# Idle products on PE, a sum among the squares, and two moves in the first stage of a two-stage kernel

## The chip, the cores and the metric

One Trainium2 chip, one of its cores. The metric is the time of one execution in microseconds on the device. The engines are PE (matrix products), DVE (vector), ACT (scalar activations), POOL (GpSimd) and SP, whose queue issues most transfers. Each has its own list of instructions, and they meet only at semaphores.

## What is computed

A block of a network on u, 16 sequences of 512 tokens with 256 channels:

```
q, k, v = u Wq + bq, u Wk + bk, u Wv + bv          # per channel, along the sequence
k = causal_conv(k, k_kernel) + k_D * k             # 512 taps per channel
y = causal_conv(k * v, ssm_kernel) + k * v * D
x = layernorm(u + (y * q) Wo + bo)
h = square(relu(x W_fc))                           # 1024 hidden
z = h W_proj                                       # back to 256
spikes: five steps of mem = 0.9 mem + z - reset, counting how often mem > 1
out = layernorm(x + count / 5)
```

## The kernel before, in words

Every float32 factor of a product is scaled by a power of two and split into a high and a low float16 part, and three products (high by high, high by low, low by high) stand for one. The scales come from maxima over weights and data.

**First stage, projections of the first 32 channels.** u comes in eight pieces. DVE takes their maxima, POOL joins them, and DVE works out the scales (`d_scale`, `read_factor`, the scaled biases `bias_b`; lines 962 to 984). ACT then makes the high part of one piece after another (semaphore `u_hi`; line 455, for pieces 5 and 7 lines 451 and 453), and DVE makes the low parts (`split_u`, line 986), POOL those of pieces 5 and 7 (line 607). PE projects the tokens in four quarters of 96 products of 96 columns each (`project`, line 684), each as soon as its two pieces are split, in turn into PSUM banks 0 to 3 and 4 to 7. DVE reads each quarter with three operations: keys (line 1000), queries (1013), values (1000), `read_projection`. After the last quarter it copies the next chunk's weights from `wnext` to `wcur` (line 1022, semaphore `wcur_ready`), for which PE and SP's next load of weights wait. `windows1` masks windows of taps (line 1040).

**Second stage, convolutions.** The 256 channels go in 32 groups of 8 (`NG`). For each group PE does a quarter of the projection of a later chunk (96 products), 96 products of the first convolution (`conv1`, line 698) and 96 of the second for the group before (`conv2`). SP loads the windows of taps of group g + 2 when half of conv1(g) is through. The first four groups are written out on PE; the others are a hardware loop over pairs (`pair_of_steps`), in which each projection stands in an If with one form and an Else with another, 96 products each, and each is followed by 96 products of conv1 and 96 of conv2. DVE ends a group with `times_q`; on the last two groups lie also the maxima of the second stage's weights `wf_st`, `wp_st` (`max_abs`, line 932).

**Between the stages.** PE transposes the joined maxima (line 883), turns the first sequence (`turn_y`, eight transposes, line 773), projects it (`project_out`, line 795, 16 recorded products), while DVE works out the scales (lines 1138 to 1149). DVE's first sums (line 1225) wait for the first half of `project_out(0)` and stand behind the scales. Their moments, POOL's root, DVE's shift, ACT's norm and PE's `turn_x` follow one another before the first sequence's products.

**Third stage, 16 sequences.** For each, PE makes eight hidden tiles (`up`, line 817, six products of 512 columns each), ACT the relu (514), DVE the square (1199), ACT its high part (518), POOL its low part (631), and PE multiplies by W_proj (`down_first`, 32 products, then `down_second`, 16; line 824). ACT's list puts the high part of tile f behind the relu of tile f + 3 (`HI_LAG`). DVE compares z with five thresholds (`spikes`, lines 1207 and 1210), for each of two halves. `second_sum` (line 1217) with its moments (1158, 1163) finishes the sequence before, and stands behind the squares and ahead of the comparisons. In the last sequence DVE makes the low parts of the odd tiles (`h_part`, line 1188). `up` for tile f waits for the relu of tile f - 2, the square of tile f in the last sequence for low part f - 4.

Of the kernel before, what the change touches and what calls it, by code (L numbers as in the profile page):

```python
# [5 lines left out]
ALU = mybir.AluOpType  # L6
# [7 lines left out]
P = 128  # L14
B, L, D, F = 16, 512, 256, 1024
NI = L // P
DT = D // P
FT = F // P
# [3 lines left out]
NC = D // CH  # L22
G = 8
GPC = CH // G
NG = D // G
# [49 lines left out]
def build(nc, uT, u, wcat, wk_n, wv_n, bias, bo, k1, k2, kd1, kd2, woT, wfT, wpT, out):  # L75
# [11 lines left out]
    with ExitStack() as ctx:  # L87
# [15 lines left out]
        w_scale = sb("w_scale", [P, 6], F32)  # L103
# [310 lines left out]
        def _(act):  # L414
# [101 lines left out]
            def hidden_hi(i, f):  # L516
                act.wait_ge(square_ready, i * FT + f + 1)
                nc.scalar.activation(h16[:, 0, f], h_square[:, f % 4], ACT.Copy).then_inc(h_hi, 1)  # L518
# [3 lines left out]
            def body(i, r, left, turn=None):  # L522
                first = isinstance(i, int) and i == 0
                if not first:
                    act.wait_ge(down_done, i * 2)
                for f in range(FT + HI_LAG):
                    if f < FT:
                        hidden_relu(i, f)
                    if f >= HI_LAG:
                        hidden_hi(i, f - HI_LAG)  # L530
                if left > 1:
                    y_turn(i + 2)
                if left:
                    if not first:
                        act.wait_ge(sum2_ready, i)
                    norm(0, i + 1, 1 - r)
                    x_turn(i + 1, 1 - r)
                if not first:
                    if turn is not None:

                        act.wait_ge(stored[1 - r], 16 * turn)
                    norm(1, i - 1, 1 - r)
# [129 lines left out]
        def _(pe):  # L672
# [17 lines left out]
            def convolve(half, out, data, taps, done):  # L690
# [11 lines left out]
                            k += 1  # L702
                last.then_inc(done, 1)

            pe.wait_ge(ld_wcur, 16)
            for quarter in range(GPC):
                pieces = (quarter + 1) * NU // GPC
# [69 lines left out]
            def turn_y(i, r):  # L777
                if isinstance(i, int) and i == 0:
                    pe.wait_ge(y_first_ready, 2)
                else:  # L780
                    pe.wait_ge(y_seq_ready, i)
                if not isinstance(i, int) or i >= 2:
                    pe.wait_ge(x_lo, i - 1)
                    pe.wait_ge(x_hi, i - 1)
                turn(y_seq[:, r], y_turned)
# [93 lines left out]
                down_second(1)  # L879

            pe.wait_ge(id_done, 3)
            pe.wait_ge(part_max2_done, 1)
            nc.tensor.transpose(ps[0:3, 4, 0:P], part_max[:, cF:cF + 3], ident[:, :]).then_inc(turned2, 1)
            turn_y(0, 0)
            pe.wait_ge(spread2, 1)
            nc.tensor.transpose(ps[:, 5, 0:3], spread_max[0:3, :], ident[0:3, 0:3]).then_inc(all_max2_done, 1)
# [18 lines left out]
        def _(dve):  # L905
            links = [0]

            def link(ins):

                links[0] += 1  # L910
                ins.then_inc(vlink, 1)
                dve.wait_ge(vlink, links[0])
# [18 lines left out]
            def max_abs(dst, src, axis=AX.XY):  # L931
                link(nc.vector.tensor_reduce(dst, src, axis, ALU.max, apply_absolute_value=True))  # L932
# [21 lines left out]
            for n in range(NU):  # L954
# [15 lines left out]
            link(nc.vector.tensor_tensor(uw, d_unscale[:, 0:1], w_unscale[:, cW:cW + 1], ALU.mult))  # L970
            nc.vector.tensor_tensor(read_factor[:, 0:1], uw, d_scale[:, 1:2], ALU.mult)

            link(nc.vector.tensor_scalar(scratch[:, 0:1], d_scale[:, 2:3], d_unscale[:, 1:2], w_unscale[:, cK1:cK1 + 1], ALU.mult, ALU.mult))
            link(nc.vector.tensor_tensor(read_factor[:, 2:3], scratch[:, 0:1], uw, ALU.mult))
            nc.vector.tensor_scalar(read_factor[:, 3:4], d_unscale[:, 2:3], w_unscale[:, cK2:cK2 + 1], uw, ALU.mult, ALU.mult)
            nc.vector.tensor_scalar(bias_b[:, :, 1], bias_b[:, :, 1], scratch[:, 0:1], None, ALU.mult)
            nc.vector.tensor_scalar(bias_b[:, :, 2], bias_b[:, :, 2], d_scale[:, 0:1], w_scale[:, cW:cW + 1],
                                    ALU.mult, ALU.mult)
            nc.vector.tensor_scalar(bias_b[:, :, 0], bias_b[:, :, 0], d_scale[:, 1:2], None, ALU.mult
                                    ).then_inc(scales2, 1)  # L980
            dve.wait_ge(scales2, 1)

            def split_u(n):
                dve.wait_ge(u_hi, n + 1)
                cols = slice(n * UP, (n + 1) * UP)
# [30 lines left out]

            def read_values(quarter, r, chunk, banks=PA):
                read_scaled(1, vbuf, quarter, r, chunk, banks).then_inc(proj_read, 1)
                if quarter == GPC - 1 and chunk + 1 < NC:

                    dve.wait_ge(ld_wnext, 16 * (chunk + 1))
                    nc.vector.tensor_copy(wcur, wnext).then_inc(wcur_ready, 2)

            def read_projection(quarter, r, n, chunk, banks=PA):
                read_keys_queries(quarter, r, n, chunk, banks)
                read_values(quarter, r, chunk, banks)
# [40 lines left out]
            for quarter in range(GPC):  # L1067
                for n in range(quarter * NU // GPC, (quarter + 1) * NU // GPC):
                    if n not in POOL_PIECES:
                        split_u(n)  # L1070
                if quarter == 0:
                    dve.wait_ge(u_lo, 2)
                if quarter == 1:
                    windows1(0, 0)
                if quarter:
                    read_projection(quarter - 1, 0, quarter - 1, 0, PAS[(quarter - 1) % 2])
            read_projection(GPC - 1, 0, GPC - 1, 0, PAS[(GPC - 1) % 2])
            windows1(1, 1)
            dve.wait_ge(u_lo, NU - len(POOL_PIECES))
# [15 lines left out]
            def times_q(s, g):  # L1095
                dve.wait_ge(c2_half, 2 * g + 2)
                q = qy[:, bass.ds(g * GC, GC)]
                nc.vector.scalar_tensor_tensor(q, PC2[:, s % 2], read_factor[:, 3:4], q, ALU.mult, ALU.mult
                                               ).then_inc(y_ready, 1)
# [20 lines left out]
                    step(s, pair * PAIR, True, pair * 2)  # L1120
            for s in range(PAIR):
                step(s, NG - PAIR, s < GPC, NC - 2)
            times_q(PAIR - 2, NG - 2)
            dve.wait_ge(ld_wf, 16)
            max_abs(part_max[:, cF:cF + 1], wf_st)
            dve.wait_ge(ld_wp, 16)
            max_abs(part_max[:, cP:cP + 1], wp_st)

# [115 lines left out]
            def body(i, r, first, last):  # L1244
                if not last:
                    first_sum(i + 1, 1 - r)
                for f in range(FT):
                    square(i, f)
                    if f == 2 and not last:
                        norm_shift(0, i + 1)  # L1250
                    if last and f in (4, 6):
                        h_part(i, f - 3)
                if last:
                    h_part(i, 5)
                    h_part(i, 7)
                if not first:
                    second_sum(i - 1, 1 - r, isinstance(i, int) and i == 1)
                spikes(i, 0, range(0, len(theta)))
                if not first:
                    norm_shift(1, i - 1)  # L1260
                if not last:
                    split_x(i + 1, 1 - r)
                spikes(i, 1, range(0, len(theta)))
# [42 lines left out]
```

## Time and profile before

| | us |
|---|---|
| median of three runs | 852.69 (850.02 to 853.04) |
| the profiled execution, its time | 849.72 |
| its span in the trace | 848.0 |
| PE busy / DVE busy / ACT busy / POOL busy | 738.3 / 710.1 / 530.8 / 384.0 |
| first product on PE | 47.02 |
| last product of the second stage on PE ends | 389.54 |
| mean granted clock of PE | 0.968 |

The span runs from the first to the last instruction of the trace, and the difference of 1.7 us lies around it. PE's products overlap one another, so that a busy share near 1 doesn't say that PE is at its peak; the granted clock says at what share of 2.4 GHz it was let run. The chain of waits goes back from the last instruction to what released each; "issue" in it is time in which an engine waited for nothing that the profile shows.

### The profile page before, as it was taken

The page shows a single profiled execution, that of the slowest core. Times are in us where ns is not written, and L with a number is a line of the kernel's source. Part 1 is how long each engine was busy: PE and PEld are TensorE (multiplying, and loading weights), DVE is VectorE, ACT ScalarE, POOL GpSimd, SP SyncE. Part 2 cuts the span into 40 slices and gives each one's busy share as a digit, 9 for nine tenths or more (in the row PEclk, how much of TensorE's full clock was granted, in tenths as well). Part 3 has the DMA queues.
Part 4 walks back from the last instruction along what each step waited for, and adds up shares of the span by engine and source line. Part 5 has one row for each costly group of instructions (what it writes and reads, how often), then busy time and mean ns, then how long its engine had stood idle before and what let it go on. Part 6 is the DMA issues. An engine that isn't in the chain of part 4 may idle for free.

```text
span 848.0 us, 26952 instructions
## 1 busy us (share of the span) xinstructions
PE 738.3 (87%) x11394; PEld 540.5 (64%) x11394; DVE 710.1 (84%) x1204; ACT 530.8 (63%) x623; POOL 384.0 (45%) x302
## 2 busy tenths in 40 slices
PE   0067977999999999876799999999999999999993
PEld 0067977999999999865455555554555555555441
DVE  6997645787788778888888999999999999999886
ACT  2383746878887888775546665566555665556661
POOL 0341212223222322224368766686666866677621
PEclk9999988999999999986999999999999999999996
DMA  8994757999999997892100111101111011100001
GB/s 335 346 259 133 178 140 166 215 226 226 222 223 229 228 221 163 176 239 75 50 0 2 51 50 50 49 0 49 49 49 44 6 49 49 49 28 22 26 25 51
DMA packets 55369, 100.71 MB, mean 119 GB/s; under 512 B 5664, under 2 KB 41376, under 8 KB 53280
## 3 DMA queue, kind: packets, MB, share of 16 engines
q1 hardware_dynamic: 53952, 97.94, 45.3%
q10 hardware_dynamic: 1376, 2.23, 0.7%
q8 instruction: 25, 0.41, 0.2%
q14 instruction: 16, 0.13, 0.1%
HBM read 89.92 MB, written 27.01 MB: 138 GB/s over the span
## 4 chain that ended last, share of the span: by engine, by line
PE 45%; DVE 24%; POOL 17%; issue 9%; DMA 2%; ACT 2%; SPq 0%; POOLq 0%; DVEq 0%; ACTq 0%
PE ps L698 17%; PE ps L684 16%; POOL arena L631 15%; DVE arena L1210 7%; PE ps L817 4%; PE ps L824 4%; DVE arena L1158 2%; DVE u_maxima L932 2%; DVE arena L1207 2%; PE ps L795 2%; DVE arena L1177 2%; DVE arena L1183 2%; POOL arena L638 1%; DMA arena<-in_wv_n 1%; DVE arena L1169 1%
## 5 line engine op out<-in xcount | busy, mean ns | idle before, releaser
L684 PE MATMUL ps<-arena 128*128 128x96 f16 x3072 | 141.9, 210 | 61.1 <-DVE arena L986 48.9
L698 PE MATMUL ps<-arena 128*128 128x64 f16 (+3 forms) x6144 | 171.7, 182 | 20.1 <-issue 9.5
L698 PEld LDWEIGHTS ps<-arena 128*128 128x128 f16 x6144 | 169.0, 97 | 21.5 <-issue 16.8
L631 POOL TENSOR_TENSOR arena<-arena 128x512 f16<-128x512 f32 x124 | 174.1, 1436 | 15.6 <-ACT arena L518 15.4
L684 PEld LDWEIGHTS ps<-arena 128*128 128x128 f16 x3072 | 137.1, 100 | 63.7 <-issue 55.9
L824 PE MATMUL ps<-arena 128*128 128x512 f16 x768 | 173.1, 379 | 3.0 <-POOL arena L631 3.0
L817 PE MATMUL ps<-arena 128*128 128x512 f16 x768 | 170.8, 379 | 2.5 <-DVE arena L1183 1.6
L595 POOL TENSOR_TENSOR arena<-arena 128x512 f16<-128x512 f32 x32 | 40.9, 1279 | 238.7 <-ACT arena L461 238.7
L1199 DVE TENSOR_TENSOR arena<-arena 128x512 f32<-128x512 f32 x128 | 136.4, 1120 | 7.5 <-POOL arena L631 6.7
L514 ACT ACTIVATE arena<-ps,read_factor 128x512 f32<-128x512 f32 x128 | 87.9, 687 | 76.9 <-PE ps L817 59.7
L824 PEld LDWEIGHTS ps<-arena 128*128 128x128 f16 x768 | 73.9, 98 | 90.7 <-POOL arena L631 9.8
L817 PEld LDWEIGHTS ps<-arena 128*128 128x128 f16 x768 | 74.2, 98 | 88.8 <-issue 3.4
L471 ACT ACTIVATE arena<-arena 64x1792 f32<-64x1792 f32 x64 | 105.2, 1688 | 17.3 <-DVE arena L1058 17.3
L466 ACT ACTIVATE arena<-arena 64x1792 f32<-64x1792 f32 x60 | 98.7, 1688 | 2.6 <-DVE arena L1040 1.8
L1210 DVE SCALAR_TENSOR_TENSOR arena<-ps,stair_at,arena 128x512 bf16<-128x512 f32 x128 | 96.1, 751 | 4.5
L518 ACT ACTIVATE arena<-arena 128x512 f16<-128x512 f32 x128 | 79.3, 623 | 29.5 <-DVE arena L1199 28.4
L502 ACT ACTIVATE arena<-arena 128x256 f32<-128x256 f32 x126 | 65.3, 589 | 38.0 <-DVE arena L1169 37.5
L635 POOL TENSOR_TENSOR arena<-arena,eps 128x4 f32<-128x4 f32 x32 | 11.6, 363 | 149.6 <-DVE arena L1163 139.3
L1058 DVE COPY arena<-arena 32x3840 f16<-32x3840 f16 x64 | 72.0, 1162 | 1.0
L795 PE MATMUL ps<-arena 128*128 128x256 f32 x256 | 60.7, 391 | 2.1 <-ACT arena L495 2.1
L461 ACT ACTIVATE arena<-arena 128x512 f16<-128x512 f32 x32 | 20.2, 630 | 62.7 <-PE ps L698 54.1
L795 PEld LDWEIGHTS ps<-arena 128*128 128x128 f32 x256 | 50.2, 197 | 10.9 <-ACT arena L495 1.4
(111 smaller groups left out, 756.2 us busy)
## 6 DMA issues: line engine op xcount, KB each, us to landing
arena<-kpad_dram SPq DMA_DIRECT2D x192, 256.0 KB, 5.7
kpad_dram<-ksplit_dram SPq DMA_DIRECT2D x64, 256.0 KB, 6.0
qy<-in_uT SPq DMA_DIRECT2D x8, 1024.0 KB, 17.2
arena<-in_u SPq DMA_DIRECT2D x16, 512.0 KB, 4.1
out<-arena SPq DMA_DIRECT2D x16, 512.0 KB, 3.0
arena<-in_k SPq DMA_DIRECT2D x2, 512.0 KB, 5.2
ksplit_dram<-arena ACTq DMA_DIRECT2D x2, 512.0 KB, 4.2
arena<-in_wfT SPq DMA_DIRECT2D x1, 1024.0 KB, 10.3
```

The source lines that it names most:

```text
L466: nc.scalar.activation(*as_pairs(*shifted(windows1_of(s, half))), ACT.Copy).then_inc(c1_copied[half], 1)
L471: nc.scalar.activation(*as_pairs(*widened(windows2_of(g, half), HP)), ACT.Copy).then_inc(c2_copied, 1)
L514: nc.scalar.activation(relu_h[:, f], PH[:, f % 2], ACT.Relu, scale=read_factor[:, 4:5]).then_inc(relu_ready, 1)
L518: nc.scalar.activation(h16[:, 0, f], h_square[:, f % 4], ACT.Copy).then_inc(h_hi, 1)
L631: nc.gpsimd.tensor_tensor(h16[:, 1, f], h_square[:, f % 4], h16[:, 0, f], ALU.subtract).then_inc(h_lo, 1)
L684: last = nc.tensor.matmul(o, u16[:, x, t, tok:tok + P], wcur[:, w, t], start=(k == 0), stop=(k == 3 * DT - 1))
L698: last = nc.tensor.matmul(out[:, ch * COL + delta * B:(ch + 1) * COL], taps(c, tp)[:, delta * P:(delta + 1) * P], data[:, xp, ch * COL:ch ...
L795: last = nc.tensor.matmul(PW[:, j // 2, (j % 2) * D:(j % 2 + 1) * D], yT[:, t, j * P:(j + 1) * P], wo[:, t], start=(t == 0), stop=(t == DT ...
L817: last = nc.tensor.matmul(PH[:, f % 2], wf16[:, w, t, f * P:(f + 1) * P], x16[:, r, x, t], start=(k == 0), stop=(k == 3 * DT - 1))
L824: return nc.tensor.matmul(PD[:, t], wp16[:, w, f, t * P:(t + 1) * P], h16[:, h, f], start=first, stop=last)
L1199: nc.vector.tensor_tensor(h_square[:, f % 4], relu_h[:, f], relu_h[:, f], ALU.mult).then_inc(square_ready, 1)
L1210: ins = nc.vector.scalar_tensor_tensor(c, y, stair_at[:, n:n + 1], c, ALU.is_gt, ALU.add)
```

## The change

- PE, ahead of the first stage: 40 products of 128 columns whose results nobody reads, into PSUM bank 7, as soon as the first high part of u is there.
- PE, between the stages: 7 such products of 512 columns into bank 5 ahead of the transpose of the maxima, and 6 behind it, ahead of `turn_y(0, 0)`.
- DVE, first stage: six scale operations, ahead of all splits until now, stand behind the first two splits; the copy of the weights stands ahead of the reads of the last quarter and waits for that quarter's products.
- DVE, end of the second stage: the maximum of `wf_st` stands ahead of the `times_q` of the group before the last.
- The last sequence: ACT puts the high part of tile f behind the relu of tile f + 1; DVE makes low parts 1, 3 and 5 behind squares 3, 5 and 7, and the sum of the sequence before with its moments behind square 3.

```diff
@@ ACT, body
-                for f in range(FT + HI_LAG):
+                lag = HI_LAG if left else 1
+                for f in range(FT + lag):
                     if f < FT:
                         hidden_relu(i, f)
-                    if f >= HI_LAG:
-                        hidden_hi(i, f - HI_LAG)
+                    if f >= lag:
+                        hidden_hi(i, f - lag)
@@ PE, ahead of the first stage
+            def idle_products(tile, n, bank, count):
+                for _ in range(count):
+                    nc.tensor.matmul(ps[:, bank, 0:n], tile[:, 0:P], tile[:, 0:n], start=True, stop=True)
+
+            pe.wait_ge(causal_done, 1)
+            pe.wait_ge(u_hi, 1)
+            idle_products(causal, P, 7, 40)
             pe.wait_ge(ld_wcur, 16)
@@ PE, between the stages
             pe.wait_ge(id_done, 3)
+            idle_products(k16[:, 0], L, 5, 7)
             pe.wait_ge(part_max2_done, 1)
             nc.tensor.transpose(ps[0:3, 4, 0:P], part_max[:, cF:cF + 3], ident[:, :]).then_inc(turned2, 1)
+            idle_products(k16[:, 0], L, 5, 6)
             turn_y(0, 0)
@@ DVE, first stage: these leave their place ahead of split_u ...
-            link(nc.vector.tensor_scalar(scratch[:, 0:1], d_scale[:, 2:3], ...))
-            link(nc.vector.tensor_tensor(read_factor[:, 2:3], scratch[:, 0:1], uw, ALU.mult))
-            nc.vector.tensor_scalar(read_factor[:, 3:4], ...)
-            nc.vector.tensor_scalar(bias_b[:, :, 1], ...)
-            nc.vector.tensor_scalar(bias_b[:, :, 2], ...)
-            nc.vector.tensor_scalar(bias_b[:, :, 0], ...).then_inc(scales2, 1)
-            dve.wait_ge(scales2, 1)
@@ ... and stand, unchanged, in the loop over the quarters
                 if quarter == 0:
+                    (the same seven)
                     dve.wait_ge(u_lo, 2)
@@ DVE, read_values
-                if quarter == GPC - 1 and chunk + 1 < NC:
+                if quarter == GPC - 1 and chunk + 1 < NC and not (isinstance(chunk, int) and chunk == 0):
@@ DVE, ahead of the last reads
+            dve.wait_ge(proj, GPC)
+            dve.wait_ge(ld_wnext, 16)
+            nc.vector.tensor_copy(wcur, wnext).then_inc(wcur_ready, 2)
             read_projection(GPC - 1, 0, GPC - 1, 0, PAS[(GPC - 1) % 2])
@@ DVE, end of the second stage
-            times_q(PAIR - 2, NG - 2)
             dve.wait_ge(ld_wf, 16)
             max_abs(part_max[:, cF:cF + 1], wf_st)
+            times_q(PAIR - 2, NG - 2)
@@ DVE, body, the last sequence
-                    if last and f in (4, 6):
-                        h_part(i, f - 3)
+                    if last and f in (3, 5, 7):
+                        h_part(i, f - 2)
+                    if last and f == 3:
+                        second_sum(i - 1, 1 - r, False)
                 if last:
-                    h_part(i, 5)
                     h_part(i, 7)
-                if not first:
+                elif not first:
                     second_sum(i - 1, 1 - r, isinstance(i, int) and i == 1)
```

## Rows read from the trace of the kernel before

**Rows 1.** The page's part 2: tenths in 40 slices of the span.
```profile
PE   0067977999999999876799999999999999999993
...
PEclk9999988999999999986999999999999999999996
```

**Rows 2.** Chain of waits, first stage: start us, us, what.
```profile
40.70 0.20 DVE scratch L973
...
42.27 4.62 DVE arena L986 x2
...
47.02 5.57 PE ps L684 x96
...
70.92 0.88 DVE arena L1022
```

**Rows 3.** Timeline, first stage: start, us, engine, line, operation [idle before <-releaser].
```profile
57.94 4.48 POOL L607 TENSOR_TENSOR arena<-qy,arena 128x2048 f16<-128x2048 f32 x1 [1.61 <-ACT arena L453]
...
60.31 4.25 DVE L986 SCALAR_TENSOR_TENSOR arena<-qy,d_scale,arena 128x2048 f16<-128x2048 f32 x1
...
68.91 0.75 DVE L1000 SCALAR_TENSOR_TENSOR arena<-ps,read_factor,arena 128x512 f32<-128x512 f32 x1 [2.21 <-PE ps L684]
```

**Rows 4.** Chain of waits, the group loop's first turns and ahead of it.
```profile
99.74 1.31 issue
101.06 1.51 PE ps L698 x37
102.57 4.82 PE ps L684 x91
107.39 0.69 issue
...
113.80 2.47 PE ps L684 x54
...
118.99 4.15 issue
...
129.81 2.09 PE ps L684 x48
...
134.33 3.99 issue
...
144.99 4.25 PE ps L684 x96
```

**Rows 5.** Chain of waits, passage between the stages and second sequence.
```profile
393.24 1.98 PE ps L773 x8
396.42 6.18 PE ps L795 x16
...
410.21 1.11 PE ps L773 x8
...
436.95 3.45 PE ps L795 x16
440.40 5.18 PE ps L817 x24
```

**Rows 6.** Timeline of DVE between the stages.
```profile
397.58 0.40 DVE L1149 TENSOR_SCALAR stair_at<-scratch 128x1 f32<-128x1 f32 x5
...
400.28 0.42 DVE L1225 TENSOR_TENSOR arena<-ps,arena 128x256 f32<-128x256 f32 x1 [2.31 <-PE ps L795]
```

**Rows 7.** Windows between the stages: busy us (instructions) by engine, granted clock.
```profile
core 0: us, PE busy (x) PEld busy (x) DVE busy (x) ACT busy (x) POOL busy (x), PEclk, DMA share, GB/s
388.00:401.00 13.00, 8.65 (x65) 6.98 (x63) 9.33 (x24) 5.09 (x4) 5.52 (x3) 0.50 0.00 0
```

**Rows 8.** Timeline of the last sequence: PE's down products, DVE's sum and comparisons.
```profile
821.72 10.52 PE L824 MATMUL ps<-arena 128*128 128x512 f16 x48
...
827.00 1.21 DVE L1217 SCALAR_TENSOR_TENSOR arena<-ps,arena 128x1024 f32<-128x1024 f32 x1
...
829.99 0.72 DVE L1207 TENSOR_SCALAR arena<-ps,stair_at 128x512 bf16<-128x512 f32 x1
```

More of the change, by code:

```diff
@@ L971, in _ @@
             nc.vector.tensor_tensor(read_factor[:, 0:1], uw, d_scale[:, 1:2], ALU.mult)
-            link(nc.vector.tensor_scalar(scratch[:, 0:1], d_scale[:, 2:3], d_unscale[:, 1:2], w_unscale[:, cK1:cK1 + 1], ALU.mult, ALU.mult))
-            link(nc.vector.tensor_tensor(read_factor[:, 2:3], scratch[:, 0:1], uw, ALU.mult))
[L975 to L980, printed above, removed]
-            dve.wait_ge(scales2, 1)
             def split_u(n):
@@ L1071, in _ @@
                 if quarter == 0:
+                    link(nc.vector.tensor_scalar(scratch[:, 0:1], d_scale[:, 2:3], d_unscale[:, 1:2], w_unscale[:, cK1:cK1 + 1], ALU.mult, ALU.mult))
+                    link(nc.vector.tensor_tensor(read_factor[:, 2:3], scratch[:, 0:1], uw, ALU.mult))
+                    nc.vector.tensor_scalar(read_factor[:, 3:4], d_unscale[:, 2:3], w_unscale[:, cK2:cK2 + 1], uw, ALU.mult, ALU.mult)
+                    nc.vector.tensor_scalar(bias_b[:, :, 1], bias_b[:, :, 1], scratch[:, 0:1], None, ALU.mult)
+                    nc.vector.tensor_scalar(bias_b[:, :, 2], bias_b[:, :, 2], d_scale[:, 0:1], w_scale[:, cW:cW + 1],
+                                            ALU.mult, ALU.mult)
+                    nc.vector.tensor_scalar(bias_b[:, :, 0], bias_b[:, :, 0], d_scale[:, 1:2], None, ALU.mult
+                                            ).then_inc(scales2, 1)
+                    dve.wait_ge(scales2, 1)
                     dve.wait_ge(u_lo, 2)
```

## The prediction, made before the changed kernel was run

> **What bounds the kernel now.** I read the page first: the row of the granted clock is full in most of its 40 slices of 21.2 us, with dips in slices 6, 7, 19 and 20 and in the last, and the row of PE's busy share is at 9 nearly throughout [rows 1]. So PE sets the pace of the two long stages, and an edit off PE's path is worth nothing there. The change touches four joints: the first stage, the code just ahead of the group loop, the passage between the stages, and the last sequence.
>
> I then read the chain of waits through the first stage. The six scale operations run from 40.70 to 42.24, ahead of the first two splits, which end at 46.89; PE's first 96 products start at 47.02 and take 5.57 us [rows 2]. At full clock the same 96 take 4.25 us, 0.0443 each [rows 4]. At the end of the stage the chain runs through the three reads of quarter 3 (68.91 [rows 3] to 70.92) and then the copy of the weights, 0.88 [rows 2].
>
> The timeline of the same stretch shows who else holds DVE. The split that starts at 60.31 lasts 4.25 us, against 2.31 for each of the first two (4.62 / 2) [rows 2, 3]. POOL's split ran from 57.94 to 62.42 [rows 3], and 62.42 + 2.15 = 64.57 is where DVE's ends: it did next to nothing until POOL was through.
>
> **First stage: scales behind the splits, 40 products ahead.** The first two splits start 1.57 us earlier (42.27 - 40.70), PE's first products at about 45.4. The scales then run 45.3 to 46.9, so splits 2 and 3 stand where they stood. The 40 idle products (128 columns each) need the first piece of u on ACT, at about 40.7. At half clock a 96-column product takes twice 0.0443, so one of 128 takes 0.118 and 40 take 4.7 us, to 45.4: they just fit. PE then finds its clock up, which saves up to 5.57 - 4.25 = 1.3 us of quarter 0. Both gains end there. Quarter 2 and quarter 3 wait for splits that end when POOL's end, and POOL waits for ACT, whose row of activations starts at the same time as now. Nothing moves POOL's 57.94, so DVE's 64.56 and the end of quarter 3 at 68.9 stay. Worth 0; if quarter 2 ran wholly at half clock, its 96 products (twice 4.25) would cost 8.5 us from 58.5 and the stage ends up to 2.5 late. Bounds -0.2 and +2.5, taken 0.
>
> A rule bears on this. The row shows the split held until POOL's ended [rows 3]. The Trainium skill, SBUF — State Buffer, section "Who interferes with whom", says that a DVE instruction with two SBUF inputs and a GpSimd instruction that reads SBUF exclude one another for the whole instruction. By sharing at half rate instead, an earlier DVE start would carry 0.2 to 0.4 us through; by the rule nothing. The trace agrees with the rule.
>
> **First stage: weights' copy ahead of the last reads.** Now: PE's quarter 3 ends, DVE reads 2.01 us (68.91 to 70.92), copies 0.88, PE goes on at 71.84. Then: DVE copies first and PE goes on at about 69.9. PE's next 96 products need only three quarters read, and write banks read long before. The reads end at 71.9, before these products do (74.2); ACT and POOL have the keys ready at 72.6; the two masks and two memsets end near 74.4, before the times-v at 76.7. So the convolution and all that its end releases (SP's window loads, spreads) move by the same 1.9. SP's wait for the copy, with the next spread queued behind it, ends earlier too. Gain 1.9; bounds 0 (cover gone) and 2.0.
>
> **Code that arrives late.** In the chain PE halts for "issue" at 99.74, 107.39, 118.99 (4.15 us) and 134.33 (3.99 us) [rows 4]. The first two halts lie 37 + 91 = 128 products apart. The third long one comes as PE leaves the first If of the group loop and jumps over the Else's 96 products; the one at 134.33 does the same in the second If. The chain's piece of 54 of 96 ends in a short halt, the second If's 48 too. From one to the other lie 384 - 6 = 378 products of code, three times 128 with 6 products' worth of waits and branches. So code comes in blocks of 128 products, one ahead. Forty products ahead move each edge 40 products back in the code: the first If now meets one after 14 products instead of 54, so the block beyond the jump is asked for 1.8 us more ahead of the jump (40 x 0.0443), and so in the second. Of the two halts of about 4 us I expect 2 us back. Against that, an edge in the third convolution falls 40 short products earlier, between loads, and costs perhaps 1 us more. Net gain 1.0; bounds 4.5 (both halts nearly gone) and -2.5 (each short halt 1 us longer). In later turns of the loop there is no such halt, so nothing follows there.
>
> **Between the stages: 7 and 6 products of 512 columns, wf's maximum ahead of times-q.** The granted clock is 0.50 from 388 to 401 us, in which PE is busy 8.65 of 13 [rows 7]; it fell before PE's last convolution was through (389.54) and rose after PE had worked unbroken from 396.42 to 401. In that time eight transposes take 1.98 and project_out 6.18 [rows 5]; at full clock they take 1.11 and 3.45 [rows 5]. DVE's first sum waits for it, until 400.28 [rows 6]. The seven products start at 389.54 with no wait. A product of 512 columns takes 0.216 at full clock (5.18 / 24 [rows 5]), so at half 0.432. No row shows when the clock would rise with the gap filled; between at once (1.5 us for the seven) and not at all (3.0) I take 2.2 us for the seven, with the clock up behind them. Then the transpose of the maxima goes at 391.8 (it waits for DVE till 391.4), six more end at 393.5, turn_y starts 0.3 late, takes 1.1 and ends 0.6 early; ACT's copy and project_out follow, whose first half is there near 397.8. DVE's scale chain ends at 397.98 (397.58 + 0.40 [rows 6]), so the sum starts at about 398.0 instead of 400.28 and saves its own later 0.25 wait on PE. All behind it hangs on it: root, shift, norm, x_hi. Gain 2.5. Bounds: 3.0, if the scale chain gains its 0.5 too; and a loss of 1, if all 13 products run at half clock (5.6 us, ending at 395.5 with the transpose among them) and only project_out is fast. The maximum of wf and times-q change places with neither waiting: both orders fill DVE from 385.9 to 391.2. Worth 0; nobody waits for that times-q before the next one. Here the rule and the sum part: the Trainium skill, TensorE: Matmul & The Clock Gate, Part 4, says that transposes don't count as activity for the clock; the trace has only eight of them at a time [rows 5] and can't show it. By the rule the products alone must carry the clock over them, as I assume.
>
> **Last sequence.** DVE's sum of the sequence before (827.00 to 830.07) stands behind all squares, and its first comparison begins at 829.99, though PE's first half of the down products (32 of the 48 that start at 821.72, 0.219 each) is there at 828.7 [rows 8]. So at most 1.3 us are to be had. Put behind square 3, the sum takes its 3.07 us while ACT waits: with the lag of one, hi 4 stands in ACT's queue ahead of relu 6 and 7, and waits for square 4 behind the sum. I get square 4 done at about 824.3, then seven DVE operations of 0.69 with one or two blocked by POOL's 1.2 to 1.3, the last lo part at 829.5 to 830.3, and PE's last product 0.2 behind it. That is the old 830. Worth 0; bounds -1.2 and +1.5.
>
> **Sum.** -1.9 - 1.0 - 2.5 = -5.4 us. The profiled execution took 849.72 with a span of 848.0, and would take 844.3 so. The three runs lie 850.02 to 853.04 with a median of 852.69, 3 us above it; off the median it is 847.3, and as the profiled one lies at the low end I say 847.0.
>
> **Rivals.** (1) Forecast, 0.5, own range 843.5 to 850. (2) The edges of the code blocks fall well and both 4 us halts nearly vanish: -1.9 - 4.5 - 2.5, 843.8 off the median; for it speaks that the block is asked for earlier, against it that DMA is about full there; 0.15. (3) The idle products do nothing but stand in the way: the clock stays at half, the gain between the stages is 0 to -1, and edges cost 1 to 2: the sum is between -2 and +1, 851 to 853; for it speaks the 4.8 us that PE worked before the clock rose at 401; 0.25. (4) Slower. The group loop now runs without halts from its second turn, so all its code stays near PE. Its end lies 48 + 96 + 192 = 336 products and some 6 of control behind an edge, 2.67 blocks; 40 and a wait more make it 2.99. If it crosses into another block and the loop no longer fits, each of its later turns pays at least one halt of 4 us: 13 x 4 = 52, 900 us or more. It decides at 3.0 blocks; 0.05. The remaining 0.05 is a small loss, to 858, from clock dips in the first stage.
>
> The Trainium skill, Runtime: NRT & Kernel Launch, section "Instruction fetch mechanics", has the same as a rule: blocks of 256 instructions fetched one ahead, and a jump outside what is held waits for a fetch. The trace agrees in the 128 products (each with its weight load) and in the 4 us; that the loop overflows no row shows.
>
> **Chances and range.** Faster by over 0.5% means below 848.4; half a per cent is about what a measurement here can tell. From (1) 0.40, (2) 0.15, a part of (3) 0.05: 0.60. Same: 0.10 + 0.20 = 0.30. Slower: 0.10. Range 842 to 852.5 leaves out the good end of (2), the top of (3) and all of (4).
>
> **What would show it.** PE's first real product at 45.4, quarter 3 still ending near 68.9; the project behind the copy at 69.9; halts on leaving the two Ifs under 3 us; 16 products of project_out in 3.5 us and the first sum near 398 less the shift; the last sequence's first comparison still about 8.3 us behind the start of its down products (829.99 - 821.72). Wrong would be: halts in every turn, or a granted clock of 0.50 under project_out.

## The result, and the profile after

The changed kernel takes 843.59 us, the median of seven runs (842.39 to 847.36), against 852.47 (849.49 to 853.20) before: ratio 0.9914, 95% interval 0.9899 to 0.9930. The ratio is taken over all executions and stands for some 7.3 us; the two medians lie 8.9 us apart. The forecast was 847.0 in a range of 842.0 to 852.5, and faster with a chance of 0.6. The profiled execution took 842.78 us with a span of 841.1, against 849.72 and 848.0. Two executions of one experiment (plus8, 946.13 and 977.62 us) were slow ones and are left out of its ratio.

To see where the time went I cut both traces at five events that both have: POOL's reduction of the maxima of u (37.43 before), DVE's first times-v (78.62), its last (381.59), PE's first up product (413.76), and the first comparison of the last sequence (829.99).

| piece, us | before | after | difference |
|---|---|---|---|
| start to POOL's reduction | 37.43 | 38.78 | +1.35 |
| to the first times-v | 41.19 | 38.64 | -2.55 |
| to the last times-v | 302.97 | 301.34 | -1.63 |
| to the first up product | 32.17 | 29.15 | -3.02 |
| to the last sequence's first comparison | 416.23 | 415.10 | -1.13 |
| to the end | 18.01 | 18.05 | +0.04 |

They add up to the 6.9 us between the spans. The first piece has no edit in it: the reduction began 0.67 us behind DVE's last maximum before and 1.82 after, with nothing that the profile names in between. In the other runs' traces this wait was 1.06 to 2.10 us, so it is scatter, and the trace of before has the shortest.

PE's busy share and the granted clock by slices of the page (answers to rows 1). The 6 that the clock had in slice 19, between the stages, is now a 9:

```profile
PE   0087877999999999977999999999999999999993
...
PEclk9999999999999999989999999999999999999997
```

The end of the first stage, from the timeline (answers to rows 3 and the copy of rows 2): POOL's split, DVE's split behind it, quarter 3 on PE, the copy, and PE's next projection.

```profile
59.28 4.48 POOL L608 TENSOR_TENSOR arena<-qy,arena 128x2048 f16<-128x2048 f32 x1 [1.62 <-ACT arena L453]
...
61.65 4.26 DVE L986 SCALAR_TENSOR_TENSOR arena<-qy,d_scale,arena 128x2048 f16<-128x2048 f32 x1
...
65.97 4.25 PE L685 MATMUL ps<-arena 128*128 128x96 f16 x96 [1.85 <-DVE arena L986]
...
70.32 0.26 DVE L1088 COPY arena<-arena 128x384 f16<-128x384 f16 x1 [2.49 <-issue]
...
70.64 3.53 PE L685 MATMUL ps<-arena 128*128 128x96 f16 x79 [0.41 <-DVE arena L1088]
```

POOL ends at 63.76, DVE's split 2.15 behind it, at 65.91, as before it ended at 64.56 behind 62.42. The copy stands where the reads stood. It takes 0.26 us instead of 0.95, and PE goes on 0.41 us behind quarter 3 instead of 2.97.

Before, the copy ran beside POOL's subtraction of the first keys:

```profile
70.40 1.26 POOL L595 TENSOR_TENSOR arena<-arena 128x512 f16<-128x512 f32 x1 [7.99 <-ACT arena L461]
...
70.83 0.95 DVE L1022 COPY arena<-arena 128x384 f16<-128x384 f16 x1
```

The halts of PE for code, from the chain of waits (answers to rows 4):

```profile
97.21 2.32 issue
...
112.86 0.77 PE ps L685 x14
113.63 1.21 issue
114.84 3.66 PE ps L685 x82
118.50 2.59 issue
...
127.16 0.39 PE ps L685 x7
127.55 1.78 issue
...
134.87 0.83 issue
...
137.66 1.25 issue
```

PE now halts after 14 products of the group loop's first If, and after 7 of the second. The halts on leaving them are 2.59 and 0.83 instead of 4.15 and 3.99, but there are others at 113.63, 127.55 and 137.66.

Between the stages, from the timeline (answers to rows 5 and 6): the last convolution's second half, the seven products, turn_y, project_out and DVE's first sum; and the same window as in rows 7.

```profile
384.85 1.41 PE L699 MATMUL ps<-arena 128*128 128x64 f16 x48 [0.55 <-ACT arena L471]
...
386.11 1.67 PE L708 MATMUL ps<-arena 128*128 128x512 f16 x7
...
390.44 1.09 PE L781 MATMUL ps<-ident,arena 128*128 128x128 f32 x8 [0.22 <-ACT arena L546]
...
392.74 3.69 PE L803 MATMUL ps<-arena 128*128 128x256 f32 x16 [0.66 <-ACT arena L495]
...
394.81 0.42 DVE L1237 TENSOR_TENSOR arena<-ps,arena 128x256 f32<-128x256 f32 x1 [0.17 <-PE ps L803]
```

```profile
388.00:401.00 13.00, 8.91 (x44) 6.68 (x45) 10.34 (x34) 6.92 (x5) 4.76 (x5) 0.95 0.13 37
```

The clock is 0.95 over these 13 us instead of 0.50; project_out takes 3.69 us instead of 6.18, and the transposes 1.09 instead of 1.98.

The last sequence (answers to rows 8): the sum, the down products, the last two low parts and the first comparison.

```profile
812.90 1.22 DVE L1229 SCALAR_TENSOR_TENSOR arena<-ps,arena 128x1024 f32<-128x1024 f32 x1
...
815.88 10.54 PE L832 MATMUL ps<-arena 128*128 128x512 f16 x48
...
819.84 2.24 DVE L1200 TENSOR_TENSOR arena<-arena 128x512 f16<-128x512 f32 x2
...
823.01 0.75 DVE L1219 TENSOR_SCALAR arena<-ps,stair_at 128x512 bf16<-128x512 f32 x1 [0.93 <-PE ps L832]
```

The low parts are done at 822.08, and DVE now waits for PE (its first half of the down products); the comparison starts 7.1 us behind the down products' start instead of 8.3.

### The profile page after: what moved, and what is told of

The parts are those of the page before. It is cut to its first block, busy times and chain, and to the rows that moved or that the text cites. A ratio compares the mean times of both kernels' runs of the same rounds, so it can differ in the third digit from the quotient of the medians.

```text
span 841.1 us, 27057 instructions
## 1 busy us (share of the span) xinstructions
PE 740.2 (88%) x11447; PEld 540.4 (64%) x11447; DVE 710.5 (84%) x1204; ACT 530.6 (63%) x623; POOL 384.2 (46%) x302
## 4 chain that ended last, share of the span: by engine, by line
PE 43%; DVE 26%; POOL 17%; issue 9%; ACT 2%; DMA 2%; SPq 0%; POOLq 0%; DVEq 0%; ACTq 0%
PE ps L699 17%; POOL arena L632 15%; PE ps L685 14%; DVE arena L1222 8%; PE ps L832 5%; PE ps L825 4%; DVE u_maxima L942 2%; DVE arena L1170 2%; DVE arena L986 2%; DVE arena L1219 2%; DVE arena L1189 2%; DVE arena L1195 2%; PE ps L803 1%; POOL arena L639 1%; DMA arena<-in_wv_n 1%
## 5 line engine op out<-in xcount | busy, mean ns | idle before, releaser
L699 PE MATMUL ps<-arena 128*128 128x64 f16 (+3 forms) x6144 | 169.5, 181 | 18.2 <-issue 8.4
L803 PEld LDWEIGHTS ps<-arena 128*128 128x128 f32 x256 | 49.6, 195 | 11.4 <-ACT arena L495 2.5
```

What stands on the lines that cost most here:

```text
L699: last = nc.tensor.matmul(out[:, ch * COL + delta * B:(ch + 1) * COL], taps(c, tp)[:, delta * P:(delta + 1) * P], data[:, xp, ch * COL:ch ...
L803: last = nc.tensor.matmul(PW[:, j // 2, (j % 2) * D:(j % 2 + 1) * D], yT[:, t, j * P:(j + 1) * P], wo[:, t], start=(t == 0), stop=(t == DT ...
```

## The experiments

Each was timed in five rounds beside the kernel before. The table cuts each profiled execution at the same events; "halts" is the sum of the "issue" pieces of 0.2 us and more in the chain between 80 and 145 us.

| run | ratio to before (interval) | to first times-v | to last times-v | to first up | to last comparison | halts |
|---|---|---|---|---|---|---|
| before | 1 | 41.19 | 302.97 | 32.17 | 416.23 | 11.9 |
| after | 0.9914 (0.9899 to 0.9930) | 38.64 | 301.34 | 29.15 | 415.10 | 12.2 |
| copy_only | 0.9946 (0.9931 to 0.9962) | 38.62 | 301.15 | 32.26 | 416.25 | 11.3 |
| mid_off | 0.9941 (0.9921 to 0.9961) | 38.61 | 303.69 | 32.32 | 415.12 | 12.0 |
| seven_only | 0.9929 (0.9907 to 0.9951) | 38.63 | 302.54 | 29.14 | 416.87 | 11.4 |
| first_off | 0.9913 (0.9898 to 0.9928) | 38.65 | 301.96 | 29.22 | 415.26 | 13.3 |
| short40 | 0.9905 (0.9887 to 0.9923) | 38.62 | 303.65 | 29.18 | 416.81 | 11.9 |
| scales_back | 0.9910 (0.9892 to 0.9928) | 38.65 | 302.78 | 30.86 | 416.42 | 12.2 |
| tail_old | 0.9904 (0.9880 to 0.9928) | 38.62 | 300.19 | 29.18 | 416.23 | 11.4 |
| plus88 | 0.9922 (0.9906 to 0.9937) | 38.64 | 301.39 | 29.17 | 415.20 | 12.4 |
| plus60 | 0.9895 (0.9870 to 0.9920) | 38.62 | 299.52 | 29.19 | 415.16 | 10.9 |
| plus3 | 0.9914 (0.9893 to 0.9934) | 38.64 | 301.49 | 29.19 | 416.87 | 11.4 |
| gap_filled | 0.9897 (0.9877 to 0.9916) | 38.62 | 301.42 | 28.59 | 415.14 | 15.0 |

The times tell little apart below 0.3%. In the traces the first column repeats within 0.04 us for all kernels with the moved copy. The column to the last times-v doesn't: it scatters by 3.5 us (300.19 to 303.69) among after, mid_off, seven_only and tail_old, which differ in nothing there. PE's granted clock from 78 to 150 us goes with it in part: it was 0.86 in mid_off, seven_only, short40 and scales_back (302.54 to 303.69) and 0.88 to 0.93 in the others (299.52 to 302.97). No verdict below rests on this column alone.

The last column has two levels for the same code: 415.1 to 415.3 in six of the kernels with the changed last sequence, and 416.4 to 416.9 in four (seven_only, short40, scales_back, plus3). The difference of 1.2 to 1.8 us is the granted clock at the start of the third stage, in these rows of after and of plus3 (the window, its length, PE's busy time and products, the granted clock, the DMA's share and GB/s):

```profile
408.00:412.00 4.00, 4.00 (x19) 1.00 0.00 0
...
408.00:412.00 4.00, 4.00 (x11) 0.50 0.00 0
```

PE works all the time in both, and gets through 19 products in one and 11 in the other. In these four traces the clock was at half for some 7 us as the first sequence's products began. It was so in none of the three without the products between the stages (before, copy_only, mid_off), where the clock had been down for some 14 us ahead of them instead.

**The copy alone (copy_only).**

```diff
--- the kernel before
-                if quarter == GPC - 1 and chunk + 1 < NC:
+                if quarter == GPC - 1 and chunk + 1 < NC and not (isinstance(chunk, int) and chunk == 0):
...
+            dve.wait_ge(proj, GPC)
+            dve.wait_ge(ld_wnext, 16)
+            nc.vector.tensor_copy(wcur, wnext).then_inc(wcur_ready, 2)
             read_projection(GPC - 1, 0, GPC - 1, 0, PAS[(GPC - 1) % 2])
```

> The kernel before with the weights' copy ahead of the last reads and nothing else. Theory: PE's project behind the copy starts 2.5 us earlier, counted from the end of quarter 3, with the copy at 0.26 us instead of 0.95 because it no longer meets POOL's subtraction; the halts in the group loop stay as they were, and 2.0 to 2.5 us faster than before, ratio 0.997 to 0.998. Rival (the halts for code are pinned to the transfers and take it back): 0 to 1 us.

Measured: 38.62 in the first column, all that the changed kernel has there, and 0.9946. The copy of the weights is the whole gain of the first stage, 2.57 us in the trace; the time shows more, 4.6 us with an interval of 3.2 to 5.9, of which the trace of this run shows 1.8 in the scattering column. Why the time shows more than the 2.57 us stays open.

**No products between the stages (mid_off), and only the seven (seven_only).**

```diff
--- the changed kernel; mid_off takes out both, seven_only the second
-            idle_products(k16[:, 0], L, 5, 7)
             pe.wait_ge(part_max2_done, 1)
             nc.tensor.transpose(...)
-            idle_products(k16[:, 0], L, 5, 6)
```

> The changed kernel without the 7 and 6 products between the stages, nothing else. Theory (they hold the clock, and project_out and the transposes run at full clock for it): the granted clock falls to 0.5 there again, project_out's 16 products take 5 to 6 us instead of 3.69, the first up products start 2 to 3 us later counted from the last convolution's end, and the whole is 3 us slower than the changed kernel, ratio to before 0.994 to 0.996. Rival (the clock stayed up in the changed kernel because of what went before, not for the products): project_out stays at 3.7 us and the time is that of the changed kernel within 0.5 us.

> The changed kernel with the 7 products ahead of the transpose of the maxima but without the 6 behind it. Theory (each gap must be kept short): with the 6 gone PE idles from 389 to 390.4 ahead of turn_y and the clock may fall under project_out in some executions; the profiled one gives either 29.2 us from the last times-v to the first up product or up to 32.3. Rival (the 7 alone carry it): 29.2 and the time of the changed kernel.

PE's rows of mid_off, the second half of the last convolution, turn_y and project_out, and the window:

```profile
386.50 1.78 PE L699 MATMUL ps<-arena 128*128 128x64 f16 x48 [0.54 <-ACT arena L471]
...
392.07 1.97 PE L781 MATMUL ps<-ident,arena 128*128 128x128 f32 x8 [1.30 <-ACT arena L546]
...
395.24 6.30 PE L803 MATMUL ps<-arena 128*128 128x256 f32 x16 [1.01 <-ACT arena L495]
```

```profile
387.00:401.00 14.00, 9.56 (x61) 7.67 (x59) 10.23 (x28) 5.99 (x4) 5.21 (x3) 0.52 0.00 0
```

The clock is down at 0.52 and the piece is 32.32 again. So the products give 3.1 us in this piece, and the rival falls. In the time they give 2.3 us (0.9941 against 0.9914), and the two intervals overlap. Part of the 3.1 us can be lost again: in four of the ten traces of the table with the seven products the clock fell under the first sequence, at a cost of 1.2 to 1.8 us (the two levels of the last column). seven_only in the same rows:

```profile
385.47 1.75 PE L699 MATMUL ps<-arena 128*128 128x64 f16 x48 [0.54 <-ACT arena L471]
387.07 2.75 PE L708 MATMUL ps<-arena 128*128 128x512 f16 x7
...
393.35 3.69 PE L803 MATMUL ps<-arena 128*128 128x256 f32 x16 [0.66 <-ACT arena L495]
```

Here the clock had fallen before the seven began (48 products of the convolution ahead of them took 1.75 us, 1.41 in the changed kernel); the seven took 2.75 instead of 1.67, and then it was up, and project_out took 3.69. The piece is 29.14: in this execution the seven did it all for this piece. Its last column is 416.87, but short40 and plus3, which have the six, show the same. The time, 0.9929, lies between the two with an interval that holds both, so whether the six are needed in some executions stays open.

**No products ahead of the first stage (first_off), or short ones (short40).**

```diff
--- the changed kernel and short40; first_off takes out all three lines of the changed kernel
             pe.wait_ge(causal_done, 1)
-            pe.wait_ge(u_hi, 1)
-            idle_products(causal, P, 7, 40)
+            idle_products(causal, 16, 7, 40)
```

> The changed kernel without the 40 products ahead of the first stage. Theory (in the first stage they are worth nothing, their worth is that the code of the group loop lies 40 products later): quarter 3 still ends 31.4 us behind the maximum's reduction on POOL, but the two halts on leaving the Ifs are about 4 us again with halts after 54 and 48 of the projections' products; 1 to 2 us slower than the changed kernel. Rival (the clock is what they bring): quarter 0 takes 5.5 instead of 4.8 us and the end of the stage or the clock later in it moves by 1 us, with the halts as in the changed kernel.

> The changed kernel with its 40 products cut to 16 columns and run early, before u is there, so that they give the clock nothing but take the same room in the code. Theory (room in the code is what counts): halts after 14 and 7 products and short halts on leaving the Ifs, as in the changed kernel, and its time within 0.5 us. Rival (the clock counts): 1 to 2 us slower, as without them.

Neither changes the first column (38.65, 38.62) or the time (0.9913, 0.9905). Without the 40, PE's first 96 products took 6.4 us, with them 4.8, and quarter 3 ended 31.45 us behind POOL's reduction in both. short40 halts after 14 products of the first If as the changed kernel does, and its halts are 11.9 us together. In first_off the halts are back where they were, as the chain shows:

```profile
111.98 2.47 PE ps L685 x54
114.45 2.69 issue
...
119.09 1.99 issue
...
131.71 4.41 issue
```

It halts after 54 products, and the two on leaving the Ifs are 1.99 and 4.41. But all halts together are 13.3 us, against 12.2, and in the time there is nothing to see. My theory had the places right and the gain wrong.

**More early products: 128 (plus88), 100 (plus60), 43 (plus3) and 48 (plus8) ahead of the first stage.**

```diff
--- the changed kernel; N = 88, 60, 3, 8
             pe.wait_ge(causal_done, 1)
+            idle_products(causal, 16, 7, N)
             pe.wait_ge(u_hi, 1)
             idle_products(causal, P, 7, 40)
```

> The changed kernel with 88 more products of 16 columns run early on PE, so that 128 products in all stand ahead of the first projection. Theory (code comes in blocks of 128 products): the edges lie where they lay before the change, halts after 54 and 48 products and of about 4 us on leaving the Ifs, 1 to 2 us slower than the changed kernel. Rival (more products simply mean later code): the halts move on and grow.

> The changed kernel with 60 more early products of 16 columns, 100 in all. Theory: the edges fall after 82 and 75 of the 96 products of the two Ifs, so that the product behind the jump lies in the block that has already come; both halts on leaving the Ifs (2.6 and 0.8 us in the changed kernel, 4.2 and 4.0 before) go, and the whole is 1 to 4 us faster than the changed kernel, ratio to before 0.987 to 0.990. Rival (the transfers hold PE up there in any case): the halts go but waits for windows take their place, same time as the changed kernel.

> The changed kernel with 3 more early products of 16 columns, 6 instructions. By the count the group loop of the changed kernel ends two to seven instructions ahead of an edge of a block of code, and 8 more products (16 instructions) took it over with 85 us lost. Theory (the edge decides and nothing else): with 6 more it lies at the edge; if it's still inside, the time is the changed kernel's, if not, 70 us or more are lost; nothing in between. Rival (the loss grows with what sticks out): some 10 to 30 us.

> The changed kernel with 8 more early products of 16 columns. By the count of products behind the edges the group loop ended some one instruction or two within its seventh block of code; now it ends 7 products into an eighth. Rival 4 of the prediction: at least one halt of 4 us in each later turn, 50 us or more slower. Theory that code stays in a larger store: no halts in later turns, time within 1 us of the changed kernel.

plus88 puts 128 products ahead, and the edges are where they were: halts after 54, and 4.19 and 4.25 us on leaving the Ifs. Together with the 37 + 91 products between two halts of before, this shows that a block holds 128 products. plus60 has its edge after 82 products:

```profile
110.81 3.66 PE ps L685 x82
...
116.10 3.48 issue
...
128.60 1.54 issue
...
131.41 2.36 issue
```

The block beyond the jump was there, as expected, but PE used it up in 16 and 10 products of it and halted for the next, 3.48 and 2.36 us. The halts move; together they are 10.9 us. Over the twelve kernels of the table with 0, 40, 43, 100 or 128 products ahead (all but gap_filled) the sum lies between 10.9 and 13.3. Where the edges lie changes little in it. That the number of blocks that the stretch needs sets it, beside the window loads, would fit, and was not tried.

plus8 takes 924.1 us, the median of four executions (920.24 to 933.05), ratio 1.087 (1.0825 to 1.0910): some 80 us more than the changed kernel. Its trace is of the execution of 977.62 us, so it shows where PE halts, and more of it than the 80 us. The chain in the loop, and the queue of the page that carries code:

```profile
162.13 5.00 PE ps L699 x192
167.12 7.69 issue
174.81 0.66 PE ps L685 x6
175.47 2.06 issue
177.54 6.17 PE ps L685 x90
...
189.70 2.08 issue
```

```profile
q8 instruction: 79, 1.29, 0.6%
```

PE halts 7.7 us at a turn of the loop and then again and again within it. Between 140 and 380 us its chain has 27 halts over 0.7 us with 64.4 us together, the changed kernel's one of 1.1. The queue carried 79 pieces instead of 25. The halts do not come in each turn: from 206.81 to 226.59 there is none, then 7.86 again. plus3, with 3 more products instead of 8, has 844.07 us, 25 pieces in that queue and no halt over 1.7 us there. So there is an edge between 43 and 48. Whether the loss beyond it grows with what sticks out is not shown, since plus3 lies inside. 100 and 128 products are free of it too, so it isn't how much code stands ahead. The loop itself is six blocks long (768 products) and some control. Counted on from the prediction's 2.99 blocks for its end, it lies in seven blocks with 0, 40, 100 or 128 products ahead and in eight with 48.

**Scales and the maximum put back (scales_back).**

```diff
--- the changed kernel: the six scale operations with their wait back ahead of split_u, and
-            dve.wait_ge(ld_wf, 16)
-            max_abs(part_max[:, cF:cF + 1], wf_st)
             times_q(PAIR - 2, NG - 2)
+            dve.wait_ge(ld_wf, 16)
+            max_abs(part_max[:, cF:cF + 1], wf_st)
```

> The changed kernel with the six scale operations back ahead of the first splits and the maximum of wf back behind times-q. Theory (both edits are worth nothing, since the splits behind them end when POOL's end, and DVE is full either way at the end of the second stage): from the maximum's reduction on POOL to the first times-v 38.6 us as in the changed kernel, from the last times-v to the first up product 29.2, time the same within 0.3%. Rival (the earlier splits help): the first figure grows by up to 1.6 us.

The first column is 38.65 and the time 0.9910: the scales' move is worth nothing. The third is 30.86 instead of 29.15, against the expectation. project_out in that trace, and a window of PE over it, with the granted clock (0.69):

```profile
393.31 5.38 PE L803 MATMUL ps<-arena 128*128 128x256 f32 x16 [0.18 <-ACT arena L495]
...
392.00:396.00 4.00, 3.02 (x9) 0.69 0.00 0
```

Up to here nothing is lost: project_out starts 13.82 us behind the last times-v, and 13.98 in the changed kernel. POOL's additions of the bias began late (385.83 against 383.74) and DVE's copy of the first sequence took 1.63 us instead of 0.61 beside them, but the maxima had ended sooner (8.90 us behind the last times-v instead of 9.61), and the two cancel. Then the clock falls under project_out, whose first half takes 3.56 us instead of 1.98, and turn_x, still at half clock, 1.39 instead of 1.11. These two make the 1.7 us. So the maximum's move is worth nothing in the time, and 0.2 us the wrong way in the trace up to project_out. Whether it has a part in when the clock falls is not shown; in the nine other traces of the table with the seven products, which all have the maximum moved, project_out took 3.69.

**The last sequence as before (tail_old).**

```diff
--- the changed kernel: lag = HI_LAG, and in DVE's body
-                    if last and f in (3, 5, 7):
-                        h_part(i, f - 2)
-                    if last and f == 3:
-                        second_sum(i - 1, 1 - r, False)
+                    if last and f in (4, 6):
+                        h_part(i, f - 3)
...     (low parts 5 and 7 and the sum behind the squares)
```

> The changed kernel with the last sequence as before it (lag of 3, sum behind the squares). Theory: the first comparison starts at 8.3 us behind the start of the down products instead of 7.1, and the whole is 1.0 to 1.1 us slower than the changed kernel. Rival (the 1.1 us came from chance in POOL's and DVE's meeting): within 0.3 us of the changed kernel.

The down products' start to the first comparison takes 8.3 us again, against 7.1 in every trace with the edit, and the piece is 416.23, that of before. So the edit gives 1.1 us. Which of its parts does it, ACT's order, the low parts or the place of the sum, was not tried apart. The time can't show it: 0.9904, no slower than the changed kernel, with an interval of 4 us.

**A version meant to be faster (gap_filled).**

```diff
--- the changed kernel: 53 early products of 16 columns, and
             (behind conv1(0))  + idle_products(u16[:, 0, 0], L, 7, 7)
             (ahead of the last turn_counts)
+            pe.wait_ge(relu_ready, B * FT)
+            idle_products(wf16[:, 0, 0], L, 4, 18)
```

> A version meant to be faster: the changed kernel with 53 early products of 16 columns (100 in all ahead of the loop with the 7 that follow), 7 products of 512 columns between the first convolution and the second group's projection, and 18 of 512 columns ahead of the last transposition of the counts. Theory: the projection at 79 us takes 4.3 instead of 5.7 us and the last eight products 0.6 instead of 1.0, so it is 1 to 2 us faster than the run with 60 early products alone, ratio to before 0.987 to 0.989. Rival (the 7 products only move the dip of the clock on): same as that run, 0.9895.

PE's rows around the first of the two new gaps, and the longest halts of the chain:

```profile
77.17 1.67 PE L708 MATMUL ps<-arena 128*128 128x512 f16 x7
79.26 4.25 PE L685 MATMUL ps<-arena 128*128 128x96 f16 x96 [0.42 <-DVE arena L1009]
```

```profile
116.93 5.00 issue
...
131.99 4.58 issue
```

The projection takes 4.25 instead of 5.65 us, and the end of the run behind the comparison 17.6 instead of 18.05. But the halts are now 15.0 us together, 2.8 more than in the changed kernel. It looks as if PE only came to the end of its code sooner; that is read off this one trace. 842.52 us and 0.9897 can't be told from plus60 (842.53) or, by the intervals, from the changed kernel. No version here is shown to beat it.

## Why the prediction was right

**The copy.** Mechanism right, term mis-sized: -1.9 forecast, -2.55 measured, above the upper bound of 2.0. I moved the copy with its duration of before, 0.88. It ran beside POOL's subtraction of the first keys (70.40 to 71.66 in the trace of before); in its new place POOL does nothing beside it, and it takes 0.26. These 0.62 us are the difference between forecast and measured. The section that I had used for the splits (the Trainium skill, SBUF — State Buffer, "Who interferes with whom") has a rule for such copies too: in a mode that uses both of DVE's ports, a copy and a GpSimd instruction block one another for the whole instruction, and the one issued first goes first. The trace agrees: the copy was issued at 70.83, behind POOL's subtraction, and ended at 71.78, 0.12 behind it. In which mode the copy ran no trace shows. I didn't apply this rule.

**Scales and 40 products.** Forecast 0, measured 0 (first_off, scales_back: 38.65 both, 38.64 with the edits), for the reason given: the splits end 2.15 us behind POOL's in both traces.

**Code that arrives late.** The blocks of 128, the edges and the shortened halts came as worked out. The step that fails is the net gain of 1.0: halts that I had priced one by one are one quantity, 10.9 to 13.3 us wherever the edges lie. The 1.63 us that this piece shows in the profiled pair is within the scatter of kernels with the same code there, so no gain is shown for the edges.

**Between the stages.** Mechanism right, -2.5 forecast, -3.02 measured, the bound that I had given for the scale chain gaining as well, which it did: it ends 15.89 us behind the last times-v instead of 16.39. The assumption that the seven start at half clock did not hold in that execution, because the clock was up as they began; where it had (seven_only) the piece was the same. What the forecast left out is that the clock can fall again behind project_out, under the first sequence: four traces lost 1.2 to 1.8 us there, the changed kernel's did not, and this was luck. (The dips that the prediction reads in slices 19 and 20 stand in 18 and 19; no number of it hangs on that.)

**The last sequence.** Forecast 0, measured -1.13 of at most 1.3. I had DVE's last low part at 829.5 to 830.3, 7.8 us or more behind the start of the down products, and it was 6.2 behind it (822.08 - 815.88), so that DVE was ready before PE. The step that fails is the time of square 4: I had it done at 824.3, 2.6 us behind the start of the down products (821.72), and it was done at 816.55, 0.7 behind it. The sum itself took its 3.07 us as forecast (812.90 to 815.97), but it began some 1.8 us earlier than that reckoning had it. From square 4 to the last low part I had 5.2 to 6.0 us, and it was 5.5. I counted seven operations there and there are six, of which POOL held two for 1.5 us each instead of 0.7.

**Sum.** The terms -2.55, -3.02 and -1.13 make -6.7, close to the 7.3 of the times; the forecast was -5.4, of which 1.0 was for halts that didn't get shorter in sum. Three steps were 0.65, 0.5 and 1.1 too small, 2.3 us together, and the 1.0 made up for part of that. The forecast time is nearer to the measured one than its steps are, and that part is luck.

**The slower rival.** It didn't come, but by how little is shown: the changed kernel's loop ends inside its last block, 3 more products are still inside and 8 more are out. The mechanism was right. The count was off by a product or more: from the 2.99 blocks that the prediction gives the changed kernel, 3 more products make 3.01, and they still fit. The price was too low, some 80 us instead of 52: in the trace of plus8 only every second turn halts, but then some eight times and not once, with 16 us in the turns from 167 to 206.

## What to carry to other kernels

Products that nobody reads are worth their place only where PE's clock would fall and real work follows on the path: between the stages 3 us, of which the clock can take more than half back a little later, and at the start nothing. A move of an operation can change its duration too, if it ran beside another engine's in the old place: here 0.95 us became 0.26. Whoever adds instructions ahead of a hardware loop should count them modulo a block of code and look at PE's turns, since three products more cost nothing here and eight more cost some 80 us.

## What the runs showed of the hardware

PE's code came in blocks of 128 products with their weight loads, and the group loop ran without long halts as long as it lay in seven blocks. With an eighth the code queue carried 79 pieces instead of 25, and PE halted in bursts in every second turn and not in each. The Trainium skill, Runtime: NRT & Kernel Launch, section "Instruction fetch mechanics", gives PE room for 2048 instructions, filled in blocks of 256. The traces agree with the block; a loop that lies in eight blocks would still fit in that room by its size, and plus8 shows that it doesn't run from it. That one of the eight must be kept for what comes next would explain it, and no run here tests that.

The halts for code in the first turns add up to 11 to 13 us whatever the edges, and in the one kernel that was made faster ahead of them (gap_filled) they were longer (15.0). That the window loads on the same transfer engines set their length fits the traces, but was not tried.
